# A selective-scan mixer: the softplus correction, the row products and the preparation of the next pair placed anew

## What is computed

```python
xz = jnp.einsum('ble,ie->bli', x, in_w)
xc, z = jnp.split(xz, 2, axis=-1)
xt = jax.lax.conv_general_dilated(xt, conv_w[:, None, :], (1,), [(DC - 1, 0)], feature_group_count=DI)
xc = _silu(jnp.transpose(xt, (0, 2, 1)) + conv_b)
x_dbl = jnp.einsum('bld,rd->blr', xc, xproj_w)
dt, Bm, Cm = jnp.split(x_dbl, [DTR, DTR + DS], axis=-1)
dt = jax.nn.softplus(jnp.einsum('blr,dr->bld', dt, dt_w) + dt_b)
dA = jnp.exp(dt[..., None] * A)
dBx = dt[..., None] * Bm[:, :, None, :] * xc[..., None]
h = dA_t * h + dBx_t            # for every token, 16 states, 256 channels
y = jnp.einsum('bds,bs->bd', h, C_t)
y = (y + xc * D) * _silu(z)     # then out_proj
```

## Time and profile before

| | us |
|---|---|
| median of 3 runs | 3914.11 |
| their range | 3894.64 to 3916.7 |
| the profiled execution | 3905.98 |
| its span, first to last instruction | 3904.1 |
| mean granted TensorE clock in it | 0.878 |

### The profile page before, as it was taken

How to read it: one execution, slowest core, us unless ns; L and a number is a source line. 1 busy time by engine, 2 the same in 40 slices (tenths; PEclk the granted TensorE clock), 3 DMA queues, 4 the chain that set the end, 5 groups by cost and what they waited for, 6 DMA issues and landing times. The chain is left out here.

```text
span 3904.1 us, 60009 instructions
## 1 busy us (share of the span) xinstructions
PE 2909.2 (75%) x18634; PEld 2118.5 (54%) x18635; DVE 2730.3 (70%) x4018; ACT 2232.2 (57%) x3990; POOL 2011.5 (52%) x1364
## 2 busy tenths in 40 slices
...
DMA packets 219678, 269.60 MB, mean 69 GB/s; under 512 B 36684, under 2 KB 139110, under 8 KB 214554
## 3 DMA queue, kind: packets, MB, share of 16 engines
...
## 5 line engine op out<-in xcount | busy, mean ns | idle before, releaser
L2009 DVE TENSOR_TENSOR_SCAN resid_x<-s_dA,resid_x 128x1024 f32<-128x1024 f32 x256 | 583.0, 2277 | 179.1 <-ACT s_dA L1826 171.4
L1735 POOL TENSOR_TENSOR resid_x<-s_ux,s_B_rows 128x1024 f32<-128x1024 f32 x256 | 606.7, 2370 | 107.5 <-PE s_y L2088 107.1
L2017 DVE TENSOR_TENSOR_SCAN resid_x<-s_back_decay,s_back_in 128x1024 f32<-128x1024 f32 x256 | 584.4, 2283 | 52.5 <-PE s_back_in L2075 52.5
L2088 PEld LDWEIGHTS s_y<-identity,resid_x 128*128 128x128 f32 x4096 | 526.8, 151 | 118.9 <-issue 83.3
L2088 PE MATMUL s_y<-identity,resid_x 128*128 128x128 f32 x4096 | 585.2, 290 | 3.8 <-POOL resid_x L1743 3.8
L1743 POOL TENSOR_TENSOR resid_x<-resid_x,s_C_rows 128x1024 f32<-128x1024 f32 x192 | 454.7, 2368 | 105.6 <-DVE resid_x L2009 105.6
L2024 DVE TENSOR_TENSOR resid_x<-resid_x,s_C 128x1024 f32<-128x1024 f32 x320 | 385.5, 1205 | 78.3 <-PE s_C L2065 76.7
L467 DVE TENSOR_REDUCE a_row_max<-a_maxscores 128x2 f32<-128x512 f32 x512 | 335.9, 683 | 77.7 <-PE a_maxscores L545 77.4
L1847 ACT ACTIVATE resid_x<-s_uT,s_bT 128x256 f32<-128x256 f32 x864 | 369.7, 495 | 5.2 <-PE s_back_in L2075 5.1
L1826 ACT ACTIVATE s_dA<-s_dt,s_A 128x510 f32<-128x510 f32 x512 | 330.1, 677 | 39.9 <-DVE resid_x L2009 39.6
L391 ACT ACTIVATE a_probs<-a_scores 128x1024 f32<-128x1024 f32 x256 | 262.7, 1026 | 142.8 <-PE a_scores L558 138.6
...
...
## 6 DMA issues: line engine op xcount, KB each, us to landing
s_B_rows<-forward_rows SPq DMA_DIRECT2D x256, 256.0 KB, 3.2
s_C_rows<-forward_rows SPq DMA_DIRECT2D x192, 256.0 KB, 3.3
...
```

Of the source, the lines that this page charges most:

```text
L1735: tt(R[s, 0], ux[par][:], brow[s % BRING][:].unsqueeze(1).broadcast_to([P, C2, W]), ALU.mult).then_inc(S["in_ready"], 1)
L2009: nc.vector.tensor_tensor_scan(r, a, r, 0.0, ALU.mult, ALU.add).then_inc(S["scanned"], 1)
L2017: nc.vector.tensor_tensor_scan(r[:, ::-1], a[:, ::-1], b[:, ::-1], 0.0, ALU.mult, ALU.add).then_inc(S["scanned"], 1)
L2088: last = mm(YP[:, t, c2 * P:(c2 + 1) * P], R[s, d][:, c2, t * P:(t + 1) * P], core.ident[:], is_transpose=True, start=(s + d == 0 and t % ...
```

## The change

- **Softplus correction.** ScalarE's instruction that subtracts 1 (L1895) and GpSimd's that subtracts e (`less_exp`) go. One VectorE scalar_tensor_tensor, `exp_less_off`, computes (ln1p - 1) - ex for 128x512, behind the backward scans of s = 3, 5, 7 and 9. The logarithm, in place, now waits for it.
- **Products.** OWN goes from (4, 6, 9, 15) to (8, 15): GpSimd has 14 of the forward products instead of 12, VectorE 2 instead of 4. CRING goes from 3 to 2. POOL_TILES goes from five states to 3, 5 and 7: ScalarE makes four more tiles per pair.
- **TensorE.** The forward `add_up` of s-1 stands behind `turn_input` of s+1 (for s = 0 it stays in front). The two directions of `bc` are split over chunks 6 and 7; bT, z, dt of the backward direction, `turn_back`, the turned input are moved by one to three chunks, with the waits on s_prep that this order needs.
- **ScalarE.** `back_decays` moves to the even chunk, ahead of the preparation there. `normed` is taken two pairs ahead, in two halves (chunks 22 and 24). The Silu block stands at the end of chunk 30, behind `decays`. The second copy of the bf16 part of the C rows is a DMA on SP's queue in slot s = 9 (the store of the B and C rows moves from slot 10 to 7).
- **GpSimd.** The preparation stands in chunks 10 to 23 instead of 7 to 22.

Cut to its core:

```diff
-BRING, CRING = 4, 3
-OWN = (4, 6, 9, 15)
+BRING, CRING = 4, 2
+OWN = (8, 15)
-POOL_TILES = {0: 2, 1: 2, 2: 2, 14: 2, 15: 2}
+POOL_TILES = {3: 2, 5: 2, 7: 2}
-PE_AT = {2: [("dt", 0, 0, k) for k in range(2)], 4: [("dt", 0, 1, k) for k in range(2)], 6: [("bc", d, k) for d in range(2) for k in range(2)],
-         7: [("bT", 0)], 8: [("z", 0)], 10: [("dt", 1, 0, k) for k in range(2)], 11: [("z", 1)],
-         14: [("dt", 1, 1, k) for k in range(2)], 20: [("uT", 0)], 25: [("uT", 1)]}
+PE_AT = {2: [("dt", 0, 0, k) for k in range(2)], 4: [("dt", 0, 1, k) for k in range(2)], 6: [("bc", 0, k) for k in range(2)],
+         7: [("bc", 1, k) for k in range(2)], 8: [("bT", 0)], 9: [("z", 0)], 10: [("z", 1)], 11: [("dt", 1, 0, k) for k in range(2)],
+         15: [("dt", 1, 1, k) for k in range(2)], 20: [("uT", 0)], 25: [("uT", 1)]}
-ACT_AT = {3: [("pre_step", 0, 0)], 4: [("exp_plus1", 0, 0)], 5: [("pre_step", 0, 1)], 6: [("ln_off", 0, 0)], 7: [("bc",)],
-          8: [("bT",), ("exp_plus1", 0, 1)], 9: [("gate", 0)], 10: [("ln_off", 0, 1)], 11: [("pre_step", 1, 0)], 12: [("gate", 1), ("exp_plus1", 1, 0)],
-          13: [("part1",)], 14: [("ln_off", 1, 0)], 15: [("pre_step", 1, 1)], 16: [("exp_plus1", 1, 1)], 18: [("ln_off", 1, 1)],
-          20: [("part2",)], 21: [("uT", 0)], 26: [("uT", 1)]}
+ACT_AT = {3: [("pre_step", 0, 0)], 4: [("exp_plus1", 0, 0)], 5: [("pre_step", 0, 1)], 7: [("exp_plus1", 0, 1)], 8: [("bc",)],
+          9: [("bT",), ("ln", 0, 0)], 10: [("gate", 0)], 11: [("gate", 1)], 12: [("pre_step", 1, 0), ("ln", 0, 1)], 13: [("exp_plus1", 1, 0)],
+          15: [("part1",)], 16: [("pre_step", 1, 1), ("ln", 1, 0)], 17: [("exp_plus1", 1, 1)], 20: [("ln", 1, 1), ("part2",)], 21: [("uT", 0)], 26: [("uT", 1)]}
+DVE_AT = {3: (0, 0), 5: (0, 1), 7: (1, 0), 9: (1, 1)}
+POOL_AT = {10: [("less_off", 0, 0), ("step_size", 0, 0)], 11: [("times_x", 0, 0)], 12: [("rest",)], 13: [("less_off", 0, 1)], 14: [("step_size", 0, 1)],
+           15: [("times_x", 0, 1)], 16: [("rest2",)], 17: [("less_off", 1, 0)], 18: [("step_size", 1, 0)], 19: [("times_x", 1, 0)],
+           21: [("less_off", 1, 1)], 22: [("step_size", 1, 1)], 23: [("times_x", 1, 1)]}
...
+                        if s == 9 and live(i, 0):
+                            sp.wait_ge(S["part1"], i + 1)
+                            sp.dma_start(bcs[u][BC:2 * BC, :], part1[:]).then_inc(S["part1_kept"], 16)
...
-                def ln_off(i, d, c):
+                def ln(i, d, c):
-                    act.wait_ge(S["plus1_done"], k + 1)
-                    func(off[:, c, :], ln1p[:, c, :], ACT.Identity, bias=Wt["minus_one"][:, 0:1]).then_inc(S["off_done"], 1)
+                    act.wait_ge(S["off_corr"], k + 1)
                     func(ln1p[:, c, :], ln1p[:, c, :], ACT.Ln).then_inc(S["ln_done"], 1)
...
+                def exp_less_off(i, d, c):
+                    k = DIRS * C2 * i + (C2 * d + c)
+                    dve.wait_ge(S["plus1_done"], k + 1)
+                    nc.vector.scalar_tensor_tensor(out=off[:, c, :], in0=ln1p[:, c, :], scalar=-1.0, in1=ex[:, c, :],
+                                                   op0=ALU.add, op1=ALU.subtract).then_inc(S["off_corr"], 1)
...
                             if s in OWN:
                                 weigh(i - 1, s, 0)
+                        if s in DVE_AT and live(i, 0):
+                            exp_less_off(i, *DVE_AT[s])
...
-                            if past:
+                            if past and s == 0:
                                 add_up(j, p, 0)
...
                                 turn_input(i, 0)
+                            if past and s:
+                                add_up(j, p, 0)
...
-                        if c in (15, 16) and live(i, 2):
-                            turn_back(i, i - 2, c - 15)
+                        if c in (13, 14) and live(i, 2):
+                            turn_back(i, i - 2, c - 13)
```

ScalarE's chunk after the change (lines that both have, and the table load that ends the Silu block, stand unmarked):

```diff
                             if s + 2 >= DS and live(i, 0):
                                 back_input(i, u, s + 2 - DS)
+                        if c % 2 == 0:
                             if s + 1 < DS and live(i, 1):
                                 back_decays(i - 1, (u + 1) % 2, s + 1)
...
-                        if c in (16, 17) and live(i, 2):
-                            turned_back(i - 2, c - 16)
+                        if c in (14, 15) and live(i, 2):
+                            turned_back(i - 2, c - 14)
...
-                        if c == 9 and live(i, -1):
-                            normed(i + 1)
-                        if c == 20 and live(i, -1):
+                        if c == 19 and live(i, -1):
                             turned(i + 1)
+                        if c in (22, 24) and live(i, -2):
+                            normed(i + 2, (c - 22) // 2)
...
-                        if c + 1 == CHUNKS:
+                        if c % 2 == 0:
+                            if s + 1 < DS and live(i, 1):
+                                decays(i - 1, (u + 1) % 2, s + 1)
...
+                        if c + 2 == CHUNKS:
                             if live(i, -1):
                                 silu(i + 1, (u + 1) % 2)
```

63 lines of the change are left out of this document (30 added, 33 removed).

## The result

The changed kernel takes 3934.94 us in the median (3913.18 to 3946.06), the kernel before 3914.98 us in the runs beside it. The ratio is 1.0053, with an interval from 1.0037 to 1.0069: half a per cent slower, where 3842 us was forecast. Its stages ahead of the mixer ran 12 us shorter than in the profile of before, though the change does not touch them. So I compare the mixer's pairs and not the spans.

The account below looks back on a forecast made before the run. Waits between in-order queues, no full engine, bound the kernel. A gain of 4.2 us in 14 pairs (-59), -3 and -2 for the last two took 3906 to 3842 us; own range 3800 to 3880, 8 in 10 3775 to 3915.

Parts of the forecast that it names:

- States 1 to 6: Scan to scan per pair: states 1 to 3 take 18.8 us, state 4 7.2, states 5 and 6 together 12.7.
- A2: Start of the forward scan of state 2, from which the prediction counted times in the pair.
- States 7 and 8: Together 14.6 us per pair, before 13.4, with 1.8 us lost to TensorE at the 1.2 GHz level.
- the walk: Engine queues followed in source order, state by state through one pair, summing to 106.9 us against 110.9.
- State 9: In time, with the correction on VectorE: 7.05 us, before 9.0.
- The forward sum, costed at nothing: TensorE's later forward sum holds GpSimd's scan input, but 6.7 us of cover before VectorE needs it makes it free.
- States 10 to 14, 15 and 0: States 10 to 14 take 29.9 us (before 31.3), 15 and 0 with the Silu block 16.6 (before 16.2).
- The filling stage: The mixer's stretch before the first gating multiply: left as it is, no gain or loss counted.
- GpSimd takes the place of the waits: GpSimd's products come 4 us late at state 9, states 10 to 15 slide: 3898 us, no change; chance 0.20.
- Slower, by decays behind a TensorE handoff with stretches at 1.2 GHz: ScalarE's decays wait in chunks 8, 12, 16; slow stretches add 7.2 us, pair 114, 3944 us; chance 0.15.
- The order works fully: All handoffs between engines in time: 101.5 us per pair, 3767 us; chance 0.12.
- The correction costs 0.62: VectorE's four corrections cost 0.62 us each: 1 us a pair gained, 3828 us; within the forecast's range, no own chance.

Follow-up runs that it names:

- one_input: The changed kernel with each VectorE correction replaced by a reduction of the same tile with one SBUF input, correction left out: 3861.6 us, ratio 0.9861.
- turns_ahead_in_before: The kernel before with one thing of the change: TensorE's forward sum of a state stands behind the turns of its backward scan: 3881.88 us, ratio 1.0034.
- yield: The changed kernel with two more GpSimd waits per pair, for the corrections of states 7 and 9 to be done: 3888.2 us, ratio 0.9915.
- correction_alone: The kernel before with only the softplus correction moved to VectorE, behind the backward scans of states 2, 4, 6 and 8: 3911.83 us, ratio 0.9994.

## Why the prediction was wrong

Two terms failed, and both were needed for the loss: the size of the corrections, and the forward sum that was costed at nothing. With either cause taken away the pair comes within 0.6 us of the forecast.

**What bounds the kernel.** Right: waits between full queues, not one engine. The waits for rows of C at 4 and 6 went away, as said, and VectorE's waits for s_C fell to 29.4 us. But they did not go at state 9: most of what is left stands there, 1.6 us a pair, where before had 0.6.

**States 1 to 6.** Right, to 0.1 us in the sum. In the pair shown above, A2 is 2336.43. The turn for state 3 starts at A2+5.63 (forecast 5.65). The second half of `bc` ends at 2351.44 + 1.93, which is A2+16.9 (17.0), and state 5 starts at 2356.09, A2+19.66 (19.7). States 5 and 6 take 12.7 (12.7). Only the split was off: the first correction takes 0.67 us, not 1.57, so states 1 to 3 take 17.8 instead of 18.8, and the wait in state 4 takes up the difference (8.1 instead of 7.2).

**States 7 and 8: the term that was mis-sized.** I took each correction at 1.57 us, start to start, with 0.62 and 1.57 as bounds. It measured 0.67, 1.64, 4.48 and 2.52. The mistake is in what the row of 1.64 was taken for: a fixed duration under contention, read where one GpSimd instruction stood beside it. The rows themselves show the hold: GpSimd's instruction ends at 3551.22 + 1.46 = 3552.68 and VectorE's at 3553.23, 0.55 us behind it. In the mixer GpSimd's instructions follow one another, and the price can reach to the next gap in its queue. That has no bound by duration, only by GpSimd's order. States 7 and 8 took 16.6 us instead of 14.6. With the reduction of 0.66 us they take 14.9 in `one_input`, so the walk through TensorE and ScalarE was about right there, and what failed for these two states is this term. The Trainium skill, page "GPSIMD Engine Reference", section "1. Specifications", which the prediction named, says that GpSimd and a VectorE instruction with two SBUF inputs contend. The trace agrees in direction, with 2.19 us against 0.66 for one input.

**State 9: a row of C that the walk left out.** I had 7.05, measured 9.1. The second row of C of state 8 stands in TensorE's queue behind a turn, the sum and `project`. I followed `turn_back` and dt through states 7 and 8, but not that row. In the pair shown that is a wait of 2.32 us, and the correction took 2.52 us instead of 1.57. In four of the thirteen pairs the correction took 0.67 us here, and state 9 took 7.04; in the others it took 9.3 to 10.4.

**The forward sum, costed at nothing: the step that failed.** I asked only whether VectorE's input from GpSimd has cover for it (6.7 us), and it nearly had: GpSimd waits 161 us more for the sums, VectorE 9 us more for its input (16.9 against 7.6), and `turns_ahead_in_before`, where GpSimd's waits grew as much, lost 1.3 us a pair in all. Two things I did not ask. The first is what TensorE does while it waits for the backward scan. In front, the sum fills that time when its input is there. Behind, it puts the preparation 0.88 us later. The second is where a later GpSimd stands when VectorE's correction comes: I counted a lateness of 5 to 6 us by state 9 as covered, and did not carry it to the corrections. It makes the one at state 7 4.5 us long instead of 2.9. With the sum in front the kernel has states 1 to 3, 4 to 6, 7 to 9, 10 to 14 and 15 with 0 in 17.8, 20.0, 22.0, 29.2 and 17.7 us. That is the walk's 106.9, at 106.7, with no stage off by more than 1.1 us. I don't count this for the walk: it was made for the other order and with corrections of 1.57 us, so that the agreement is in part luck.

**States 10 to 14, 15 and 0.** 31.4 instead of 29.9, 17.4 instead of 16.6. Of the 31.4, 1.2 us belong to the hold (`one_input` has 30.2) and 2.2 to the sums (29.2 with them in front; the two overlap and don't add). The 0.8 us at 15 and 0 are the same in `one_input`. They don't come from the correction; no run took them apart further.

**The filling stage** was left as it is, and rightly: from the mixer's start to the first gating it is 199.2 us, before 198.1.

**The rivals.** *GpSimd takes the place of the waits*: its wait grew to 268.3 us, as the signs of this rival say. By itself this costs little; its lateness came back through the longer hold, which this rival does not have. *Slower, by decays behind a TensorE handoff with stretches at 1.2 GHz*: the time came out between this rival's 3944 and the forecast, nearer to it. Its sign, states 7 and 8 over 17, was missed by 0.4, and state 4 stayed under 9.2. A slow stretch behind a handoff was there: the transposes of `turn_back` at 2483.66, after 2.23 us of idle time, end in a stretch at 0.50 to 0.66 of the clock. A second one stands behind VectorE's hold. But `one_input` has this order of the decays too and takes 107.5 us, and putting the decays first in chunks 8 and 16 changed the pair of `yield` by 0.1 us, in six chunks by 0.7. So the right side with a wrong mechanism. *The order works fully* (101.5 us) never came: with both cures the pair takes 106.9, which fits the waits on TensorE's own work that spoke against it. *The correction costs 0.62*: `one_input` gives this, and in the order of after it is worth 5.5 us a pair, not 1; in the good order nothing.

**The chances.** Nine tenths of 0.53 is 0.48, not 0.50; "faster by over 1%" should have been 0.62, not 0.64. Nothing hangs on it.

**Left open.** Whether the hold costs anything in the kernel before is not shown, since `correction_alone` also takes work off two engines. Its 3.2 us make state 4 longer by 2.8 (12.7 + 5.5 + 8.2 us for states 4 to 6, against 9.9 + 6.2 + 8.8); part of this comes back at 5 and 6 and the rest at states 7 to 9 (19.7 against 21.8). Open too is which changes of GpSimd's instructions let the correction in without a gap.
